# Expert tiles of a routed FFN: each scatter adds its rows to one array of token sums in DRAM, one behind the other, and the sums are copied to the output

## The reference, cut to what matters

```python
rn = (xf - mu) * jax.lax.rsqrt(var + EPS) * ln_gamma + ln_beta
probs = jax.nn.softmax(rn @ gate_w.T, axis=-1)
rw, sel = jax.lax.top_k(probs, K)                      # K = 2 of E = 8
comb = jnp.sum(jax.nn.one_hot(sel, E) * rw[..., None], axis=1)
h = jax.nn.gelu(jnp.einsum('nc,efc->enf', xf, w1), approximate=False)
y = jnp.einsum('enf,ecf->enc', h, w2)
out = jnp.einsum('enc,ne->nc', y, comb)
x = x + out                                            # xf: the layernormed x, 2048 tokens
```

## Time and profile before

| | us |
|---|---|
| median of 3 runs | 1112.41 (1108.83, 1112.41, 1122.13) |
| the profiled execution | 1115.67 |
| its span, first to last instruction | 1113.6 |
| TensorE matmuls busy in the span | 998.8 (90%) |
| VectorE busy | 778.7 (70%) |
| ScalarE busy | 651.8 (59%) |
| GpSimd busy | 498.9 (45%) |
| mean granted TensorE clock | 0.961 of full speed |

### The profile page before, as it was taken

One profiled execution on the slowest core, in us unless ns is written; L12 is line 12 of the kernel. 1 busy time (PEld: TensorE's weight loads), 2 busy tenths in 40 slices (PEclk: granted clock), 3 DMA queues, 4 the chain that ended last, 5 costly groups with the idle time before them and its releaser, 6 DMA issues.

```text
span 1113.6 us, 17009 instructions
## 1 busy us (share of the span) xinstructions
PE 998.8 (90%) x5550; PEld 630.9 (57%) x5550; DVE 778.7 (70%) x1755; ACT 651.8 (59%) x874; POOL 498.9 (45%) x550
## 2 busy tenths in 40 slices
PE   8889999989877999999999798999997887999991
PEld 3345444434466888878877563444432333888881
DVE  7767788887778778888877148788868844444443
ACT  4357667666656786776866615676655650555550
POOL 6558897896414435336344501215141634222220
PEclk9899999999889999999999899999989988999996
DMA  7854979648999700000003402575544347222216
GB/s 247 226 180 159 294 205 352 192 146 276 226 216 218 144 1 1 1 2 1 1 29 87 118 16 86 156 214 132 164 106 114 88 153 278 62 65 74 72 57 226
DMA packets 74200, 149.87 MB, mean 135 GB/s; under 512 B 7823, under 2 KB 44577, under 8 KB 72580
## 3 DMA queue, kind: packets, MB, share of 16 engines
q1 hardware_dynamic: 61380, 98.80, 34.4%
q0 software_dynamic: 10800, 47.63, 12.0%
q10 hardware_dynamic: 1936, 2.36, 0.7%
HBM read 73.14 MB, written 76.25 MB: 134 GB/s over the span
## 4 chain that ended last, share of the span: by engine, by line
PE 62%; ACT 13%; DVE 11%; issue 5%; DMA 4%; POOL 4%; SPq 1%; ACTq 0%; DVEq 0%; POOLq 0%
PE ps L1318 14%; PE ps L1452 10%; PE ps L1433 7%; PE ps L1418 5%; PE ps L1637 4%; PE ps L1402 4%; PE ps L1392 3%; ACT pt L1105 3%; PE ps L1660 3%; PE ps L1623 3%; DVE negmax L1859 2%; ACT pt L1184 2%; DVE pt L2205 2%; PE ps L1461 2%; PE ps L1783 1%
## 5 line engine op out<-in xcount | busy, mean ns | idle before, releaser
L1859 DVE TENSOR_REDUCE negmax<-ps 128x2 f32<-128x1024 f32 x256 | 309.8, 1222 | 59.7 <-PE ps L1418 55.0
L1105 ACT ACTIVATE pt<-ps 128x1024 f32<-128x1024 f32 x256 | 259.2, 1027 | 139.6 <-PE ps L1433 136.5
L1452 PE MATMUL ps<-pt,v_aug 128*32 128x512 f32 x1024 | 143.8, 623 | 4.1 <-POOL pt L804 3.2
L1433 PE MATMUL ps<-sq,sk 57*128 57x512 f32 (+1 forms) x512 | 128.4, 499 | 6.3 <-DMA sq<-m_sb 3.7
L1418 PE MATMUL ps<-sk,sq 56*128 56x512 f32 (+1 forms) x512 | 107.9, 425 | 23.8 <-ACT pt L1105 18.8
L804 POOL TENSOR_TENSOR pt<-pt,near 128x256 f32<-128x256 f32 x128 | 92.4, 730 | 50.8 <-ACT pt L1105 50.2
L1433 PEld LDWEIGHTS ps<-sq,sk 57*128 57x128 f32 (+1 forms) x512 | 48.9, 188 | 105.6 <-issue 68.7
L996 POOL DMA_INDIRECT expert_out<-yo,dest x39 | 38.1, 976 | 117.6 <-ACT yo L1285 102.7
L1623 PE MATMUL ps<-sel,hl 128*128 128x512 f32 x256 | 74.0, 423 | 17.2 <-DVE pt L2205 11.5
L1418 PEld LDWEIGHTS ps<-sk,sq 56*128 56x128 f32 (+1 forms) x512 | 49.5, 190 | 45.5 <-ACT pt L1105 31.7
L2327 DVE TENSOR_TENSOR ghl<-ps,ghl 128x512 fp32r<-128x512 f32 x39 | 27.0, 692 | 60.7 <-ACT ghl L1278 60.7
(11 more groups left out here) (323 smaller groups left out, 2044.6 us busy)
## 6 DMA issues: line engine op xcount, KB each, us to landing
expert_rows<-zero SPq DMA_DIRECT2D x3, 5586.0 KB, 62.5
expert_weights_split<-wst POOLq DMA_DIRECT2D x8, 2048.0 KB, 8.4
qk_rows<-hl SPq DMA_DIRECT2D x30, 512.0 KB, 3.0
sk<-qk_rows SPq DMA_DIRECT2D x62, 192.0 KB, 4.7
sq<-qk_rows SPq DMA_DIRECT2D x62, 192.0 KB, 4.3
moe_w<-in_w POOLq DMA_DIRECT2D x16, 512.0 KB, 8.0
wexp<-expert_weights_split POOLq DMA_DIRECT2D x16, 512.0 KB, 5.4
wexp<-expert_weights_split SPq DMA_DIRECT2D x4, 2048.0 KB, 14.1
```

The costliest lines, as they stand in the source:

```text
L1105: act.activation(pt[:, 4 * (U % 2) + 2 * half:4 * (U % 2) + 2 * half + 2, :], ps[:, bank:bank + 2, :], ACT.Exp, scale=(BIAS, SCALE)[L]).th ...
L1433: ins = pe.matmul(ps[:, key.bank + s, :], sk[r, pair, c * P:(c + 1) * P], sq[r, pair, :], start=True, stop=True)
L1452: ins = pe.matmul(ps[32 * j:32 * j + 32, OBANK, :], v_aug[:, b % 2, c, HG * g + j, :], pt[:, 4 * (U % 2) + j, :], start=(c == 0), stop=(c ...
L1859: dve.tensor_reduce(negmax[:, n % 2, col:col + 9:8], ps[:, job.bank:job.bank + 2, :], AX, ALU.max, negate=True).then_inc(s_jd, 1)
```

## The change

The array `yg` with its two rows per token goes. In its place stands `acc` (`token_sums`), one row per token and 128 rows behind them for padding. It is filled with `x_tok`: batches 0 to 2 by SyncE during attention of layer 1, each behind a wait on `s_ln3`, batch 3 behind the load of the first `xr`; the 128 spare rows are zeroed. A scatter now adds its rows to those in DRAM (`compute_op=ALU.add`). Since two scatters may hold rows of the same token, each waits for the landing of the one before. A padding row goes to spare row 2048 + its place, so all 128 rows of every tile are written. `dest` is a maximum of two numbers, one VectorE instruction less. At the end SyncE copies `acc` to the output in four DRAM to DRAM transfers; the reads, the eight additions and the stores out of SBUF are gone.

```diff
--- before.py
+++ after.py
@@ -315,7 +315,7 @@
         rows = nc.dram_tensor("qk_rows", (2, B, 4, 3, P, T), F32, kind="Internal").ap()
 
         xg = nc.dram_tensor("expert_rows", (XROWS, XW), F32, kind="Internal").ap()
-        yg = nc.dram_tensor("expert_out", (2 * NTOK, D), F32, kind="Internal").ap()
+        acc = nc.dram_tensor("token_sums", (NTOK + P, D), F32, kind="Internal").ap()
         wx = nc.dram_tensor("expert_weights_split", (ME, P, EW), F32, kind="Internal").ap()
 
         w_first = sb("w_first", [P, 4, KC, D])
@@ -431,9 +431,8 @@
         yo = sb("yo", [P, 3, D])
         mix = sb("mix", [P, ME])
         wsel = sb("wsel", [P, NTILE])
-        second = sb("second", [P, NTILE])
+        spare = sb("spare", [P, 1])
         dest = sb("dest", [P, NTILE], U32)
-        yfin = wexp[:, 0:4 * 2 * TT * D].bitcast(F32).rearrange("p (a i t d) -> p a i t d", a=4, i=2, t=TT)
 
         flat = lambda v: v[:].rearrange("p i t -> p (i t)")
         simcat = [xnT[:, i, :] for i in range(2)]
@@ -512,7 +511,7 @@
         s_up = sem("up_psum"); s_gelu = sem("gelu_ready"); s_t2 = sem("gelu_turned")
         s_gh = sem("gelu_hi"); s_gl = sem("gelu_split"); s_dn = sem("down_psum")
         s_meta = sem("tile_rows_out"); s_y = sem("y_scaled"); s_yo = [sem(f"y_sent{i}") for i in range(3)]
-        s_yin = [sem(f"y_in{i}") for i in range(4)]; s_fin = sem("out_ready")
+        s_acc = sem("sums_started")
         s_o = sem("out_stored")
         s_own = sem("dve_own")
 
@@ -609,6 +608,9 @@
                             load_stacks(L, b, (u + STACKS[b]) // 4)
                         if b + 2 < B and u == NEXT_CTX[L][b]:
                             load_ctx(L, b + 2)
+                        if L and b < B - 1 and u == 25:
+                            sp.wait_ge(s_ln3, TT * (b + 1))
+                            sp.dma_start(tokens(acc[T * b:T * (b + 1), :]), x_tok[:, b]).then_inc(s_acc, 16)
 
             sp.dma_start(x_tok[:, 0], tokens(a["x"][0])).then_inc(s_x[0], 16)
             load_ctx(0, 0)
@@ -651,6 +653,7 @@
                 n = XROWS // P
                 k0, k1 = n * i // 4, n * (i + 1) // 4
                 sp.dma_start(xg_rows[:, k0:k1, :], zero[:].unsqueeze(1).broadcast_to([P, k1 - k0, XW])).then_inc(s_zero, 16)
+            sp.dma_start(acc[NTOK:NTOK + P, :], zero[:, 0:D]).then_inc(s_acc, 16)
             first_rows()
             attention(1)
 
@@ -667,16 +670,14 @@
                     sp.wait_ge(s_t1, j - 2)
                     sp.wait_ge(s_meta, j - 2)
                 sp.dma_start(xr[:, j % 3, :], xg[bass.ds(row, P), :]).then_inc(s_xr[j % 3], 16)
-
-            sp.wait_ge(s_dn, NTILE)
+                if j == 0:
+                    sp.wait_ge(s_ln3, TT * B)
+                    sp.dma_start(tokens(acc[T * (B - 1):T * B, :]), x_tok[:, B - 1]).then_inc(s_acc, 16)
+
             for i in range(3):
                 sp.wait_ge(s_yo[i], 16 * len(range(i, NTILE, 3)))
             for b in range(B):
-                for i in range(2):
-                    sp.dma_start(yfin[:, b, i], tokens(yg[NTOK * i + T * b:NTOK * i + T * (b + 1), :])).then_inc(s_yin[b], 16)
-            for b in range(B):
-                sp.wait_ge(s_fin, b + 1)
-                sp.dma_start(tokens(out[b]), x_tok[:, b]).then_inc(s_o, 16)
+                sp.dma_start(out[b].rearrange("(p k) d -> p (k d)", p=P), acc[T * b:T * (b + 1), :].rearrange("(p k) d -> p (k d)", p=P)).then_inc(s_o, 16)
             sp.wait_ge(s_o, 16 * B)
 
 
@@ -993,8 +994,12 @@
                     pool.wait_ge(s_tile, 1)
                 pool.wait_ge(s_meta, j + 1)
                 pool.wait_ge(s_y, j + 1)
-                pool.indirect_dma_start(yg, bass.IndirectOffsetOnAxis(ap=dest[:, j:j + 1], axis=0), yo[:, j % 3, :], None,
-                                        bounds_check=2 * NTOK - 1, oob_is_err=False).then_inc(s_yo[j % 3], 16)
+                if j == 0:
+                    pool.wait_ge(s_acc, 16 * (B + 1))
+                else:
+                    pool.wait_ge(s_yo[(j - 1) % 3], 16 * ((j - 1) // 3 + 1))
+                pool.indirect_dma_start(acc, bass.IndirectOffsetOnAxis(ap=dest[:, j:j + 1], axis=0), yo[:, j % 3, :], None,
+                                        bounds_check=NTOK + P - 1, oob_is_err=True, compute_op=ALU.add).then_inc(s_yo[j % 3], 16)
 
 
         @block.scalar
@@ -2163,7 +2168,8 @@
                 own_wait(dve.tensor_tensor(past8, is_e[:], per_tile(cnt[:], ME), ALU.mult))
                 own_wait(dve.tensor_reduce(tile_n[:], past8, AX, ALU.add))
                 own_wait(dve.scalar_tensor_tensor(out=skip[:], in0=tile_s[:], scalar=col("row"), in1=tile_n[:], op0=ALU.add, op1=ALU.is_ge))
-                own_wait(dve.tensor_scalar(skip[:], skip[:], float(4 * NTOK), None, ALU.mult))
+                own_wait(dve.tensor_scalar(spare[:], col("row"), float(NTOK), None, ALU.add))
+                own_wait(dve.tensor_scalar(skip[:], skip[:], spare[:], None, ALU.mult))
 
             dve.wait_ge(s_x[0], 16)
             stats(0, x_tok[:, 0], range(TT))
@@ -2331,9 +2337,8 @@
                 if j == 0:
                     own.wait()
                 own(dve.tensor_tensor(mix[:], x[:, D:D + ME], is_e[:, j, :], ALU.mult))
-                own_wait(dve.tensor_scalar(second[:, j:j + 1], x[:, D + ME + 1:D + ME + 2], tile_e[:, j:j + 1], float(NTOK), ALU.not_equal, ALU.mult))
-                own(dve.scalar_tensor_tensor(out=dest[:, j:j + 1], in0=second[:, j:j + 1], scalar=x[:, D + ME:D + ME + 1], in1=skip[:, j:j + 1],
-                                             op0=ALU.add, op1=ALU.add))
+                own_wait(dve.scalar_tensor_tensor(out=dest[:, j:j + 1], in0=skip[:, j:j + 1], scalar=x[:, D + ME:D + ME + 1], in1=skip[:, j:j + 1],
+                                                  op0=ALU.max, op1=ALU.max))
                 own_wait(dve.tensor_reduce(wsel[:, j:j + 1], mix[:], AX, ALU.add))
                 dve.sem_inc(s_meta, 1)
 
@@ -2344,11 +2349,6 @@
                 if j + 1 < NTILE:
                     tile_low(j + 1)
                 gelu_low(j)
-
-            for b in range(B):
-                dve.wait_ge(s_yin[b], 32)
-                own_wait(dve.tensor_tensor(x_tok[:, b], x_tok[:, b], yfin[:, b, 0], ALU.add))
-                dve.tensor_tensor(x_tok[:, b], x_tok[:, b], yfin[:, b, 1], ALU.add).then_inc(s_fin, 1)
 
 
 def layout(i):
```

## The result

The changed kernel is slower: 1150.1 us median (1144.8 to 1157.9) against 1110.6 for the kernel before in the same comparison, ratio 1.036 (95% interval 1.031 to 1.040), or +39.5 us. The forecast was 1125 (+12.6), the range 1101 to 1160: the time lies inside it, but the change is three times the one forecast.

A forecast was written before the change was run, and what follows sets the result against it. TensorE was taken to set the tile pace and transfers the end; chain +13.3, late scatters +6.4, last scatter +1.0 and end -8.1 sum to +12.6 us on the 1112.4 median, forecast 1125 us, range 1101 to 1160.

The forecast's parts named there:

- What bounds the kernel: Last 161 us: TensorE alone sets the tile pace of 3.65 us until the scatters finish, then transfers set the end.
- The threshold: Scatter stage: a landing of 2.81 us is the point from which the chain is no longer hidden behind TensorE.
- 1. The chain of scatters: Scatter stage: each scatter waits for the landing before, a step of 4.0 us against 3.65 per tile, +13.3 us.
- The longer burst: Within a scatter's landing: reading the sums from DRAM lengthens the packets by 0.4 us if overlapped, 0.9 if in turn.
- rule of two read descriptors: Scatter transfers: a reducing transfer emits two read descriptors per chunk, doubling 0.39 us of engine time; step 3.63 us.
- the first rival: Scatter stage: reads overlap, the step stays at or below 3.65 us, 1105 us in all; chance 0.28.
- 2. Late scatters: Scatter stage: four late landings, 3.6 to 4.2 us, are paid in full in a chain without slack, +6.4 us.
- 3 and 4. The last scatter and the end: After the last tile: written padding makes the last landing later, +1.0 us; copies shorten the end to 11.4 us, -8.1.
- 5 and 6. Filling the sums, VectorE: 0.: Filling the sums in attention delays nothing, and dropping one 207 ns VectorE instruction per tile gains nothing: 0 us each.
- The hidden chain: Scatter stage: landing below 2.8 us, so TensorE still sets the pace; 1102 to 1107 us, chance 0.28.
- The dear one: Scatter stage: every adding scatter lands after 4.2 us, step 5.04, +47 us, 1159 us; chance 0.28.
- The feared fall of the clock: Scatter stage: with TensorE busy only 72% of a tile, a lower granted clock could come on top; no size given.

The follow-up runs named there:

- experiment 1: The changed kernel with plain scatters in place of adding ones, keeping the waits, the filling and the final copies: 1100.7 us, ratio 0.992 to the kernel before.
- experiment 2: The changed kernel with two arrays of sums, each scatter waiting for the one before the last, only the first array copied out: 1103.4 us, ratio 0.993.
- experiment 7: The changed kernel, waiting for the scatter just before only where the tile's expert changes (first three always wait), padding rows skipped: 1104.6 us, ratio 0.992 to the kernel before.
- the second profile: The changed kernel run once more, nothing altered, to get another profile: 1151.1 us, ratio 1.037 to the kernel before.

## Why the prediction was wrong, point by point

*What bounds the kernel.* Right: the pace of a tile was TensorE's, the slack of a chain 0.41 us, the end a matter of transfers. The threshold too held: experiment 1, whose chained landings take 2.4 us, stays at 3.65, experiments 2 and 7, where most scatters don't wait for the one just before, at 3.62 and 3.64, and kernels whose landings chain above 2.8 us don't.

*1. The chain of scatters.* This is the step that failed, by its size. I put the step of the chain at 4.0 us, hence +13.3, with 6.4 us for late scatters beside it: 19.7 in all. The chain cost 43.7. At the medians the step is 3.83 + 0.84 = 4.67 us, which alone is 38 x (4.67 - 3.65) = +38.8 where I had 13.3. Three terms made up my step. The 0.84 us from landing to the next start: right, 0.84 was measured. The longer burst: I had +0.4 (overlapped) to +0.9 (in turn), and 0.82 was measured, so the serial end was the right one, and I went below it. GpSimd's instruction: the text said it could only grow, and gave that growth no number of its own; it is 0.57 us, all of it on the path, since the first packet comes 0.57 us later. 3.24 + 0.57 + 0.82 = 4.63, within 0.04 of the step. The prediction named growth of this instruction as a sign that it was wrong, and that sign came. A size named as "can only grow" should have gone into the sum with a bound, and the middle between two ends was no place to stand when the unpriced term pushed only one way. Why the instruction takes longer when it adds, no run here shows.

The Trainium skill's rule of two read descriptors for a reducing transfer, as the prediction cites it from "Collectives: The Full Stack", gave a step of 3.63 and the first rival. For these scatters it was too low: 1.13 us of engine time in place of 0.39 is a factor of 2.9 and not 2, with 144 packets in place of 48. The doubling, moreover, was applied to transfer time alone, and of the 1.4 us by which a landing grew 0.57 came ahead of the first packet.

*2. Late scatters.* I added 6.4 us for four late landings. They didn't come as such: the latest was 4.4 us (4.6 in the second profile), 0.6 to 0.8 above the median, where I had up to 1.8. But many small excesses came: the mean step is 4.80 (mean landing 3.90, 0.89 to the next start), 0.13 above the step at the medians, which over 38 steps is 5 us. The size was near, the shape wasn't.

*3 and 4. The last scatter and the end.* +1.0 and -8.1, together -7.1; measured +1.7 and -10.1, together -8.4 (-8.3 in the second profile). The copies take 9.4 us from issue to the end, I had 11.4: their packets run from 1.4 to 8.6 us after the first issue, 7.2 us for the 2.10 MB, nearer to the 5.5 of a one-sided transfer than to the 10.9 of a shared rate. The 9.8 us that the prediction works out from the Trainium skill was too slow for them as well. The padding tiles, which are now written too and which I had inside the step, have a price by experiment 7's landings of 2.7 us: if padding were skipped, the last three steps and the last landing would each be shorter by about 1.1 us, an estimate of 4 us of the loss.

*5 and 6. Filling the sums, VectorE: 0.* Right, as far as the runs tell: with the filling the first scatter starts at 952.7 us in the second profile, without it at 953.3 in the kernel before. The L613 transfers were issued at 766.95, 830.17 and 894.95, each before the next L573 (772.96, 835.32, 899.71), as read from the rows.

*The rivals.* The hidden chain didn't come (landing 3.8, not 2.8). The dear one asked for 5.04; the outcome lies at 4.80, beyond the point of 4.25 from which it is slower by 2%, so it is nearer to the dear case than to the forecast. The feared fall of the clock hardly came with it: TensorE busy 85% between 953 and 1085 us, granted clock 0.98. In one stretch, 1005 to 1011 us, it was 0.72, and the scatters kept their distance through it (1004.24, 1008.77 and 1013.36), so it isn't the clock that sets this pace.

## What to carry to other kernels

A wait that orders one transfer behind another turns latency into pace: before it is added, the sum is landing + time to the next start, against the pace of the loop, and here 2.8 us of landing were allowed and 3.8 came. Changing what a DMA does (a copy into an addition) changed three things at once here, the length of GpSimd's instruction, the number of packets and the time that they keep the engines busy, and each needs its own number. Where an order is needed only between some neighbours, waiting there alone kept all of the gain at the end (experiment 7); a wait whose value comes out of a table cost nothing that shows, with a distance of 3.64 us; GpSimd had idle time for it.

## What the runs showed of the hardware

- An adding scatter of 128 rows of 1 KB from SBUF to DRAM: GpSimd 1.55 us (plain 0.98), landing 3.8 us (plain 2.4), 144 packets (plain 48), 1.13 us of all 16 engines (plain 0.39). The engine time fell to 0.72 us for half the bytes and to 0.60 for half the rows, which also have half the bytes.
- Apart from 16 packets of 4 bytes, the adding scatter has one packet for each row (128 of 1 KB; 64 with half the rows), the plain one 32 of 4 KB.
- The first packet of a scatter comes 0.57 us after the end of GpSimd's instruction, whether that takes 0.98, 1.41 or 1.55 us.
- Where a scatter starts before the one ahead has landed, it lands later: 4.2 us in experiment 2, 4.0 in experiment 7, where scatters follow each other every 3.6 us.
- Four DRAM to DRAM copies of 512 KB end 9.3 to 9.4 us after the issue of the first.
- From a landing to the start of the next scatter on GpSimd pass 0.84 us (median of the changed kernel), as from a ScalarE semaphore (0.84 in the earlier trace rows).
